# Re-ordering the five queues of a quantised matmul with a layernorm, a base linear layer and LoRA experts, with 83 operations given to another engine

## What is computed

```python
def fake_quant(x, scale, zp):
    q = jnp.clip(jnp.round(x / s + z), QMIN, QMAX)
    return (q - z) * s
x = x + jnp.matmul(fake_quant(_layernorm(x), ...), fake_quant(ctx_4096, ...))
y = _layernorm(x)
base = y @ W_base.T + b_base
lora_out = jnp.einsum('ter,eor,te->to', h, lora_B, w) * SCALING   # h = y @ lora_A, w: top 2 of 8 experts
x = x + base + lora_out
```

## Time and profile before

| | |
|---|---|
| median of 3 runs | 960.43 us (956.87 to 961.31) |
| the profiled execution | 960.41 us, span 958.6 us, granted clock 0.996 |
| TensorE busy | 931.6 us, 97% |
| VectorE busy | 585.5 us, 61% |
| ScalarE busy | 506.9 us, 53% |
| GpSimd busy | 310.2 us, 32% |
| DMA | 197.08 MB, mean 206 GB/s |

### The profile page before, as it was taken

The page is one execution under the profiler, slowest core; times in us unless marked ns, Lnnn a source line. Parts: engine busy times, 40 slices in busy tenths (PEclk is TensorE's granted clock), DMA queues, the critical chain, the costliest instruction groups (busy, mean ns, idle before and its releaser), DMA issues. The chain is left out here.

```text
span 958.6 us, 13081 instructions
## 1 busy us (share of the span) xinstructions
PE 931.6 (97%) x4594; PEld 443.1 (46%) x4614; DVE 585.5 (61%) x729; ACT 506.9 (53%) x495; POOL 310.2 (32%) x249
## 2 busy tenths in 40 slices
...
GB/s 345 412 412 393 219 376 298 299 255 307 293 67 181 198 243 209 221 146 242 200 211 276 181 223 188 345 308 214 117 22 116 50 93 72 98 123 75 85 66 44
DMA packets 61445, 197.08 MB, mean 206 GB/s; under 512 B 5696, under 2 KB 22208, under 8 KB 52928
## 3 DMA queue, kind: packets, MB, share of 16 engines
...
## 5 line engine op out<-in xcount | busy, mean ns | idle before, releaser
L1470 PE MATMUL PS<-XA,Q 128*128 128x512 f16 x384 | 145.6, 379 | 0.0
L1472 PE MATMUL PS<-XA,Q 128*128 128x512 f16 x384 | 145.5, 379 | 0.0
L1471 PE MATMUL PS<-XA,Q 128*128 128x512 f16 x384 | 145.5, 379 | 0.0
L1428 POOL TENSOR_TENSOR S<-S 128x1024 f16<-128x1024 f32 x29 | 64.6, 2233 | 169.4 <-ACT S L1422 169.4
L694 PE MATMUL PS<-Q,S 128*128 128x512 bf16 x501 | 112.7, 383 | 2.2 <-DVE S L709 1.3
L694 PE MATMUL PS<-EX,S 128*128 128x512 bf16 (+1 forms) x535 | 105.7, 354 | 3.5 <-POOL S L674 1.6
L1422 ACT ACTIVATE Q<-S 128x1024 f16<-128x1024 f32 x64 | 66.6, 1050 | 73.2 <-PE PS L1472 29.5
L1470 PE MATMUL PS<-EX,S 128*128 128x512 f16 x256 | 97.0, 379 | 0.5 <-ACT Q L1532 0.5
L1471 PE MATMUL PS<-EX,S 128*128 128x512 f16 x256 | 97.0, 379 | 0.0
L1472 PE MATMUL PS<-EX,S 128*128 128x512 f16 x256 | 97.0, 379 | 0.0
L1377 ACT ACTIVATE S<-S,WC 128x1024 f32<-128x1024 f32 x64 | 70.7, 1137 | 46.1 <-DMA S<-in_wT_dram 31.4
...
## 6 DMA issues: line engine op xcount, KB each, us to landing
...
```

The lines of the kernel that those rows point to most:

```text
L1428: e.tensor_tensor(v[:, 1024:2048], W_SRC[n], v[:, 0:1024], ALU.subtract).then_inc(w_lo.of(i, n), 1)
L1470: e.matmul(bank(bk), wh, yh(op, k), start=(fresh and k == 0), stop=False, skip_group_check=not fresh)
L1471: e.matmul(bank(bk), wh, yl(op, k), start=False, stop=False, skip_group_check=not fresh)
L1472: last = e.matmul(bank(bk), wl, yh(op, k), start=False, stop=(read and k == 7), skip_group_check=not fresh)
```

## The change

sync_first (the first loads) stays. Behind it the queues of all five engines are written in a new order, and 83 operations change engine: w_low (27 from GpSimd to VectorE, 6 the other way), y_low (4 and 17), sqadd0 3, 5, 7 and add0 3, 7, 9 to VectorE, add0 4, 5 to GpSimd; ctx_conv 6, 12, 15, 16, 18, 21, 30 from ScalarE to GpSimd, 4 and 24 from GpSimd and 10 from VectorE to ScalarE; ctx_quant 6 and 10 from ScalarE to VectorE; ln1_back(0,3,0) and (1,4,0) and ln1_quant(1,5) from ScalarE to VectorE, and ln1_back(1,1,0), (1,2,0), (1,5,0), (1,6,0), (1,7,0) and ln1_quant(1,4) from VectorE to ScalarE. No call is added or left out, and TensorE's instructions are the same 4,570 in another order. Two lines shorter, the new file's lines from tensor_program on stand two earlier. The diff, cut:

```diff
-QUANT = {'a': [(0, 0), (0, 2), (0, 3), (0, 4), (0, 5), (0, 6), (0, 7), (1, 1), (1, 2), (1, 3), (1, 5), (1, 6), (1, 7)],
-    'd': [(0, 1), (1, 0), (1, 4)]}
-BACK = {'a': [(0, 0, 0), (0, 1, 0), (0, 2, 0), (0, 3, 1), (0, 3, 0), (0, 4, 0), (0, 5, 0), (0, 6, 0), (0, 7, 0), (1, 0, 0),
-    (1, 3, 0), (1, 4, 0)], 'd': [(0, 7, 1), (1, 1, 0), (1, 2, 0), (1, 5, 0), (1, 6, 0), (1, 7, 0)]}
-CTXQ = {'a': [0, 3, 6, 7, 8, 9, 10, 11, 12, 13, 14, 15, 16, 17, 19, 18, 20, 21, 22, 23, 24, 25, 26, 28, 27, 29, 30, 31],
-    'd': [1, 2, 4, 5]}
-CONV = {'a': [5, 6, 8, 9, 12, 13, 14, 15, 16, 17, 18, 21, 22, 25, 26, 27, 28, 29, 30, 31], 'd': [10, 11, 23], 'p': [0, 1, 2, 3,
-    4, 7, 19, 20, 24]}
+QUANT = {'a': [(0, 0), (0, 2), (0, 3), (0, 4), (0, 5), (0, 6), (0, 7), (1, 1), (1, 2), (1, 3), (1, 4), (1, 6), (1, 7)],
+    'd': [(0, 1), (1, 0), (1, 5)]}
+BACK = {'a': [(0, 0, 0), (0, 1, 0), (0, 2, 0), (0, 3, 1), (0, 4, 0), (0, 5, 0), (0, 6, 0), (0, 7, 0), (1, 0, 0), (1, 1, 0),
+    (1, 2, 0), (1, 3, 0), (1, 5, 0), (1, 6, 0), (1, 7, 0)], 'd': [(0, 3, 0), (0, 7, 1), (1, 4, 0)]}
+CTXQ = {'a': [0, 3, 7, 8, 9, 11, 12, 13, 14, 15, 16, 17, 18, 19, 20, 21, 22, 23, 24, 25, 26, 28, 27, 29, 30, 31], 'd': [1, 2, 4,
+    5, 6, 10]}
+CONV = {'a': [4, 5, 8, 9, 10, 13, 14, 17, 22, 24, 25, 26, 27, 28, 29, 31], 'd': [11, 23], 'p': [0, 1, 2, 3, 6, 7, 12, 15, 16,
+    18, 19, 20, 21, 30]}
...
-SQ0 = {'d': [], 'p': [1, 2, 3, 4, 5, 6, 7, 8, 9, 10, 11, 12, 13, 14, 15]}
-SUM0 = {'d': [4, 5], 'p': [1, 2, 3, 6, 7, 9, 10, 11, 12, 13, 14, 15]}
...
-    (1, 7, '4'), (1, 7, 'T')], 'p': [(0, 0, 'A'), (0, 0, 'T'), (0, 1, 'A'), (0, 2, 'T'), (0, 3, 'T'), (0, 4, 'A'), (0, 6, 'T'),
-    (0, 6, 'A'), (1, 2, 'T')]}
...
-    (15, 5)], 'p': [(0, 6), (0, 2), (0, 5), (1, 2), (1, 5), (1, 6), (2, 2), (2, 6), (2, 5), (3, 2), (3, 5), (3, 6), (4, 2),
-    (4, 6), (5, 2), (5, 6), (6, 2), (6, 6), (7, 6), (7, 2), (8, 1), (8, 0), (8, 4), (8, 2), (8, 3), (8, 6), (8, 5), (9, 3),
-    (9, 2), (10, 2), (10, 3), (11, 3), (11, 2), (12, 2), (12, 3), (13, 3), (13, 2), (14, 3), (14, 2), (15, 2), (15, 3)]}
...
+SQ0 = {'d': [3, 5, 7], 'p': [1, 2, 4, 6, 8, 9, 10, 11, 12, 13, 14, 15]}
+SUM0 = {'d': [3, 7, 9], 'p': [1, 2, 4, 5, 6, 10, 11, 12, 13, 14, 15]}
...
+    (1, 5, '4'), (1, 5, 'T'), (1, 6, 'A'), (1, 6, 'B'), (1, 7, 'A'), (1, 7, 'B'), (1, 7, 'T')], 'p': [(0, 0, 'T'), (0, 0, 'A'),
+    (0, 1, 'T'), (0, 2, 'A'), (0, 2, 'T'), (0, 3, 'A'), (0, 4, 'T'), (0, 4, 'A'), (0, 5, 'A'), (0, 5, 'T'), (0, 7, 'A'),
+    (1, 0, 'A'), (1, 0, '4'), (1, 0, 'B'), (1, 0, 'T'), (1, 2, '4'), (1, 2, 'B'), (1, 2, 'T'), (1, 4, 'B'), (1, 6, '4'),
+    (1, 6, 'T'), (1, 7, '4')]}
...
+    (14, 5), (15, 1), (15, 3), (15, 2), (15, 0), (15, 5), (15, 4), (15, 6)], 'p': [(0, 0), (1, 0), (1, 2), (3, 5), (4, 0),
+    (4, 3), (4, 2), (4, 6), (5, 2), (5, 6), (6, 6), (7, 0), (7, 1), (7, 2), (7, 6), (8, 0), (8, 5), (9, 2), (10, 2), (12, 2)]}
...
-        xn_load(e, 0, 4); xn_load(e, 0, 5); ctx_load(e, 2); xn_load(e, 0, 6); xn_load(e, 0, 7); x_load(e, 0, general)
-        x_load(e, 1, general); xn_load(e, 1, 0); x_load(e, 2, general); ctx_load(e, 3); x_load(e, 5, general)
-        xn_load(e, 1, 1); ctx_load(e, 4); xn_load(e, 1, 2); x_load(e, 6, general); ctx_load(e, 5); x_load(e, 3, general)
-        ctx_load(e, 6); xn_load(e, 1, 3); x_load(e, 9, general); x_load(e, 4, general); xn_load(e, 1, 4); ctx_load(e, 7)
-        r_load(e); ctx_load(e, 8); keep(e, 3); x_load(e, 7, general); xn_load(e, 1, 5); ctx_load(e, 9)
-        x_load(e, 8, general); ctx_load(e, 10); xn_load(e, 1, 6); ctx_load(e, 11); x_load(e, 10, general); ctx_load(e, 12)
-        x_load(e, 12, general); x_load(e, 11, general); keep(e, 2); ctx_load(e, 13); xn_load(e, 1, 7); ctx_load(e, 14)
-        keep(e, 7); keep(e, 0); ctx_load(e, 15); x_load(e, 15, general); keep(e, 1); ctx_load(e, 16); keep(e, 6); keep(e, 5)
...
-        b_load(e, 15); raw_load(e, 15, 0); ob_load(e, 0); ob_load(e, 1); last_store(e, 4); last_store(e, 5)
-        last_store(e, 3); last_store(e, 6)
+        xn_load(e, 0, 4); xn_load(e, 0, 5); ctx_load(e, 2); xn_load(e, 0, 6); xn_load(e, 0, 7); x_load(e, 1, general)
+        x_load(e, 0, general); xn_load(e, 1, 0); ctx_load(e, 3); x_load(e, 2, general); ctx_load(e, 4); xn_load(e, 1, 1)
+        x_load(e, 3, general); x_load(e, 5, general); xn_load(e, 1, 2); ctx_load(e, 5); x_load(e, 7, general)
+        ctx_load(e, 6); xn_load(e, 1, 3); x_load(e, 4, general); ctx_load(e, 7); xn_load(e, 1, 4); x_load(e, 9, general)
+        ctx_load(e, 8); x_load(e, 6, general); x_load(e, 8, general); keep(e, 2); ctx_load(e, 9); xn_load(e, 1, 5)
+        ctx_load(e, 10); x_load(e, 11, general); keep(e, 1); ctx_load(e, 11); x_load(e, 10, general); keep(e, 5)
+        x_load(e, 15, general); xn_load(e, 1, 6); ctx_load(e, 12); ctx_load(e, 13); keep(e, 0); x_load(e, 14, general)
+        x_load(e, 13, general); r_load(e); x_load(e, 12, general); x_load(e, 17, general); ctx_load(e, 14); ctx_load(e, 15)
...
+        raw_load(e, 15, 1); raw_load(e, 15, 0); ob_load(e, 0); ob_load(e, 1); last_store(e, 5); last_store(e, 4)
+        last_store(e, 6); last_store(e, 3)
...
-        gemm1(e, 9, 512, 1024, 0, 8); gemm1(e, 9, 0, 512, 0, 8); gemm1(e, 9, 0, 512, 8, 16); ln1_turn(e, 1, 4)
...
-        gemm1(e, 16, 0, 512, 8, 16); gemm1(e, 16, 512, 1024, 8, 16); a_total(e); mean(e, 0); gemm1(e, 17, 0, 512, 0, 8)
-        gemm1(e, 17, 512, 1024, 0, 8); r_total(e); gemm1(e, 17, 0, 512, 8, 16); gemm1(e, 17, 512, 1024, 8, 16)
-        gemm1(e, 18, 0, 512, 0, 8); gemm1(e, 18, 512, 1024, 0, 8); offset_total(e, 0); offset_total(e, 1)
...
-        gemm1(e, 31, 0, 512, 8, 16); lora_h(e, 0, [0]); w_total(e, 0); lora_h(e, 0, [1]); lora_h(e, 0, [2])
-        lora_h(e, 0, [3]); lora_h(e, 0, [4]); lora_h(e, 0, [5]); lora_h(e, 0, [6]); lora_h(e, 0, [7])
...
+        gemm1(e, 6, 512, 1024, 0, 8); gemm1(e, 6, 0, 512, 8, 16); ln1_turn(e, 1, 4); gemm1(e, 6, 512, 1024, 8, 16)
...
+        gemm1(e, 17, 0, 512, 0, 8); mean(e, 0); a_total(e); gemm1(e, 17, 0, 512, 8, 16); r_total(e)
+        gemm1(e, 17, 512, 1024, 0, 8); gemm1(e, 17, 512, 1024, 8, 16); offset_total(e, 0); gemm1(e, 18, 0, 512, 0, 8)
+        gemm1(e, 18, 0, 512, 8, 16); offset_total(e, 1); gemm1(e, 18, 512, 1024, 0, 8); var_total(e, 0, 0)
+        var_total(e, 0, 1); gemm1(e, 18, 512, 1024, 8, 16); gemm1(e, 19, 0, 512, 0, 8); gemm1(e, 19, 512, 1024, 0, 8)
...
+        w_total(e, 0); lora_h(e, 0, [1]); lora_h(e, 0, [2]); lora_h(e, 0, [3]); lora_h(e, 0, [4]); product(e, 0, 0, 0, 1)
+        product(e, 0, 0, 1, 2); product(e, 0, 0, 2, 3); product(e, 0, 0, 3, 4); product(e, 0, 0, 4, 5); lora_h(e, 0, [5])
+        lora_h(e, 0, [6]); product(e, 0, 0, 5, 6); product(e, 0, 0, 6, 7); product(e, 0, 1, 0, 1); clear(e, 0)
+        lora_h(e, 0, [7]); product(e, 0, 0, 7, 8); mean(e, 1); route(e, 0); product(e, 0, 1, 1, 2); product(e, 0, 3, 0, 1)
...
-        ln1_quant(e, 0, 3); ln1_back(e, 0, 2, 0); ln1_back(e, 0, 3, 1); ln1_back(e, 0, 3, 0); ln1_quant(e, 0, 4)
...
-        post(e, 1, 2); square1(e, 8); post(e, 1, 1); w_squares(e, 2); w_scale(e, 2, 0); w_scale(e, 2, 3); w_scale(e, 2, 2)
...
-        w_high(e, 7, 5); post(e, 7, 2); a_high(e, 1, 0); a_high(e, 1, 1); w_scale(e, 8, 2); w_scale(e, 8, 0)
...
+        square0(e, 0); square0(e, 1); square0(e, 2); square0(e, 3); ctx_conv(e, 10); ctx_quant(e, 12); square0(e, 4)
...
+        w_high(e, 1, 5); copy(e, 1); w_high(e, 1, 6); square1(e, 6); post(e, 1, 2); square1(e, 7); post(e, 1, 1)
...
+        y_high(e, 1, 7, "T"); y_high(e, 1, 7, "4"); post(e, 7, 2); w_scale(e, 8, 2); w_scale(e, 8, 3); w_high(e, 7, 5)
...
+        add0(e, 7); ln1_quant(e, 1, 5); shift0(e, 0); shift0(e, 1); ln1_stats(e, 1, 6); shift0(e, 2); shift0(e, 3)
...
-        y_scale(e, 0, 3, "A"); y_diff3(e, 0, 3); evac1(e, 25, 0); y_diff1(e, 0, 3); evac1(e, 25, 1); add1(e, 9)
...
-        y_diff2(e, 0, 7); y_low(e, 0, 7, "B"); y_diff4(e, 0, 7); y_low(e, 0, 7, "A"); y_low(e, 0, 7, "4"); w_low(e, 0, 0)
-        w_add(e, 0, 1); y_low(e, 0, 7, "T"); lora_sums(e, 0); w_low(e, 0, 1); w_add(e, 0, 2); w_add(e, 0, 4); centre1(e, 0)
...
-        centre1(e, 8); w_norm(e, 2); w_seen(e, 2); w_factors(e, 2); post(e, 1, 4); centre1(e, 9); w_add(e, 2, 1)
...
+        y_scale(e, 0, 7, "A"); y_diff3(e, 0, 7); y_diff1(e, 0, 7); y_diff2(e, 0, 7); w_add(e, 0, 1); y_low(e, 0, 7, "B")
+        y_diff4(e, 0, 7); b_low(e, 0); y_low(e, 0, 7, "4"); y_low(e, 0, 7, "T"); w_low(e, 0, 1); w_add(e, 0, 2)
+        w_add(e, 0, 4); w_low(e, 0, 4); w_low(e, 0, 2); lora_sums(e, 0); w_low(e, 0, 6); centre1(e, 0); w_low(e, 0, 3)
...
+        w_norm(e, 2); w_seen(e, 2); w_factors(e, 2); post(e, 1, 4); centre1(e, 9); w_add(e, 2, 1); w_low(e, 2, 0)
...
-        add0(e, 3); ln1_coef(e, 1, 4); ctx_conv(e, 7); ln1_coef(e, 1, 5); add0(e, 6); add0(e, 7); sqadd0(e, 1); sqadd0(e, 2)
-        sqadd0(e, 3); sqadd0(e, 4); sqadd0(e, 5); sqadd0(e, 6); sqadd0(e, 7); sqadd0(e, 8); ln1_coef(e, 1, 6); add0(e, 9)
...
```

(36 more changed lines are left out.)

549 lines of the change are left out of this document (256 added, 293 removed), and 73 rows, old and new, of tables (EVAC, GEMM, POST, PROD).

## The result

The changed kernel takes 965.61 us (median of 10 executions, 960.13 to 969.4) where the one before takes 960.50 (956.87 to 963.74): a ratio of 1.0059, 95% interval 1.0031 to 1.0086. It is 5 us slower where 5.8 us less had been forecast, and it lies outside the range. The profiled execution took 963.62 us with a span of 961.8, 3.2 more than before's 958.6.

A forecast was written before the change was run, and what follows sets the result against it. TensorE was taken as the bound, busy in 931.6 of 958.6 us. Gains of 9.2 less costs of 3.4 gave 5.8 net, so 960.4 − 5.8 = 954.6 us; range 950.5 to 965, the forecast case's own 951.5 to 958.

The forecast's parts named there:

- All else costs nothing, by cover: Remaining engine moves (w_low, y_low, conversions, sums) in context stretch and products: no cost, as the queues have time to spare.
- The clock, 2.8 us of gain: TensorE's low clock at 160 to 190 and 360 to 370 was to be won back: 1.1 and 1.7 us.
- The second dip: Clock of 0.83 from 360 to 370, taken as gone with the gap directly before it: 1.7 us gained.
- The first, 1.1: Clock of 0.89 and 0.97 at 160 to 190, two chances in three of going as one-column matmuls are spread: 1.1 us.
- the last sign of being wrong: The prediction would be wrong if the clock fell at a new place, 1.7 us each.
- The waits at 365, 285 and 599: TensorE's waits for a norm of W, a low part of y and a post step go: 2.3, 1.2 and 0.7 us gained.
- 160 and 230: TensorE's waits for ctx_conv(18) and for eviction evac1(25,1) go: 0.5 and 1.3 us gained.
- the costs of 71 to 102 and 279 to 293: Context stretch with xn_load(1,6) queued later: 1.1 us (0 to 12); w_low(0,0) on GpSimd: 1.2 us (0 to 3).
- Lead-in 0.3, tail 0.4: ln1_back(0,3,0) ends later on VectorE: 0.3 us; a second last-store issue lies behind the last eviction: 0.4 us.
- The starving DMA: Rival: SP's queue between 70 and 100 starves the context stretch of DMA, 965 to 969 us; chance 0.15.
- The lock: Rival: y_low on GpSimd, 430 to 480, holds off VectorE's two-input operations through shared ports, costing 3 to 5 us; chance 0.14.
- The third rival: The order changes nothing that binds, each wait finds its next releaser: 959 to 961 us; chance 0.05.

The follow-up runs named there:

- e1_stores: Changed kernel with store(7,0) and store(7,1) moved behind w_low(8,0) and w_low(8,5) in GpSimd's queue: 961.18 us, 1.002 against the kernel before.
- e8_stores_mid: Changed kernel with store(7,0) and store(7,1) behind w_low(8,0) only, ahead of w_low(8,5): 960.32 us, 1.0016 against the kernel before.
- e9_stores_tail: Changed kernel with the stores as in e1_stores and last_store(3) ahead of last_store(6) again: 960.82 us, 1.0011 against the kernel before.
- g3: As g2, with store(7,0) and store(7,1) behind w_low(8,5): 963.21 us, 1.0023 against the kernel before.
- g2: Kernel before up to 335 us, then the new order and engines, the two early stores among them: 967.51 us, 1.0081 against the kernel before.
- a0_after: The changed kernel itself measured once more, nothing edited: 967.73 us, 1.009 against the kernel before.
- e5: Kernel before with one edit, store(0,0) ahead of w_low(1,5) in GpSimd's queue: 959.56 us, 1.0007 against the kernel before.
- e5b: Kernel before with store(0,0) ahead of w_low(1,5), measured a second time: 958.47 us, 0.9995 against the kernel before.
- g1: Changed kernel's queues and engines up to 337 us, then the order and engines of before: 961.15 us, 1.0009 against the kernel before.

## Why the prediction was wrong, step by step

The forecast was 5.8 us less and 5.1 more came, 10.9 apart. Two things make it up. One is the cost of two stores, 4.3 to 6.5 us between medians; the other is that the gains did not show in the time: with those stores held back (e1_stores, e8_stores_mid, e9_stores_tail) the new order is 1 to 2 us above the kernel before, not 5.8 below. TensorE's waits of 0.3 us and more, behind the first 30 us, sum to 7.8, 5.6 and 3.9 us in the profiles of these three, and to 5.7 and 7.9 in two profiles of before. The waits that were booked went, and others of about the same size came in their place.

- **The step that failed: "All else costs nothing, by cover"**. The prediction itself says that what changes behind 600 can only lose, and then puts that loss at nothing. It counted the w_low that leave GpSimd by their own durations and asked whether they had time. It did not ask what stood behind them in that queue. Six w_low of block 8 had held stores (7,1), (6,1) and (7,0) back until all y loads but the last had landed; with five of them gone and the sixth behind the stores, two stores of 512 KB share the DMA engines with loads that TensorE is about to want. Price: 2.5 to 4.3 us of waiting in the five profiles that have it, 4.3 to 6.5 us between medians (e1_stores against the changed kernel, g3 against g2). That the stores do it is shown by e8_stores_mid: y_load(2) lands 3.8 us sooner with the stores later and all else equal, and the delay is then on y_load(4). How the DMA engines divide their time between the two is not shown. The medians differ by more than the wait; part of that is the clock. In the profiled execution the low clock behind the wait adds some 1.7 us (15 × 0.08 + 5 × 0.11), in that of a0_after nothing; in the mean of all executions the clock costs 2.2 us in the changed kernel against 1.1 with late stores. The rest is not settled.
- **The clock, 2.8 us of gain: wrong as a sum.** The mean granted clock costs the kernel before 2.1 to 2.6 us (1 minus the clock, times 960, in four sets of 16 to 29 executions beside the experiments) and the changed one 2.2 (14 executions). The second dip, 1.7, was one execution's: the clock in 360 to 370 was 1.00 in the second profile of before, and e5 and e5b, which take away the wait there, still cost 2.2 to 2.5. The first, 1.1, may well have come: with the new context stage and without the early stores (e1, e8, e9 and g1, 42 executions) the clock costs 1.1 us, some 1 less than before. In the changed kernel the early stores bring as much back, and the clock fell at a new place, behind the wait at 627, as the last sign of being wrong had it. Which edit of the context stage does it is not shown.
- **The waits at 365, 285 and 599: gone, as predicted.** None of them is over 0.5 us in a profile of the changed kernel or of e1, e8 and e9. At 365 w_squares(2) of the changed kernel starts at 358.2, not behind a post but behind a raw load that landed just then, where before it started at 360.2. That raw load is the next releaser, which the prediction did not price: in g2 and g3, with the new order from 335 but the old context stage, it lands 1 to 2 us later, and the wait at 365 is 3.0 and 2.7 us, more than the 2.1 of before. So the order of the products does not take the wait away by itself. Also the 2.3 us were one execution's (1.4 in the second profile of before), and e5 and e5b show that taking the wait away alone gives nothing that 24 executions can tell.
- **160 and 230, and the costs of 71 to 102 and 279 to 293:** in sum wrong. The waits at 160 and 230 are gone in both profiles of the changed kernel, and the 1.2 at 279 to 293 did not come as a wait. By 337 the changed kernel was to be 1.9 us ahead (3.4 of waits and 1.1 of clock won, 2.6 spent); TensorE was 2.0 late there in the profile. The wait at 103 was 1.55 us where 1.1 had been allowed, lateness at 115 was 1.9. Not foreseen were 1.56 at 204 (keep(19) queued behind two context loads, its landing at 198.8, x_load(21) behind it) and 0.7 each at 247 and 269. Over executions g1 puts the whole stage at 0.9 us dearer, with an interval of −1.4 to +3.3.
- **Lead-in 0.3, tail 0.4:** TensorE went on at 29.42 instead of 29.27 with a wait of 1.81 for 1.39; the tail cost 0.8.
- **Rivals.** The starving DMA was the right resource at the wrong place: the waits near 103 were small, but the landing of a load hurt at 627. The lock cost TensorE nothing that shows: VectorE's y_low (the form of 23 before, 17 after) has a mean of 1278 ns against 1221, w_low 1268 against 1244, and w_total waits 0.2 us. Single hits there are, 12 two-input operations of VectorE over 1.7 us beside one of GpSimd, 9 before; one falls into 430 to 480, a w_add of 3.04 us at 460.9, where three were feared. The third rival, that each wait finds its next releaser, had 0.05; with late stores it describes what was measured, and in the changed kernel itself the stores come on top.

```profile
L1031 DVE TENSOR_TENSOR S<-S 128x1024 f16<-128x1024 f32 x17 | 21.5, 1278 | 1.3 <-ACT S L992 0.8
...
L1428 DVE TENSOR_TENSOR Q<-S,Q 128x1024 f16<-128x1024 f32 x52 | 65.6, 1268 | 45.1 <-ACT Q L1422 45.1
L1428 POOL TENSOR_TENSOR Q<-S,Q 128x1024 f16<-128x1024 f32 x12 | 26.6, 2220 | 46.8 <-ACT Q L1422 46.8
```

**Left open:** why e1_stores, e8_stores_mid and e9_stores_tail, whose profiles lack before's waits at 285, 365 and 599, still come out 1 to 2 us above it (each interval holds no difference). In the mean their clock costs some 1 us less than before's, so something else must take 2 to 3 us more, an estimate from the two. Part is seen: waits of 0.5 to 1.9 us for the evictions of groups 30 and 31 at 267 to 272, and 0.4 for the gates (the weights w of the experts, which tail waits for) at 324 to 331. What else comes in their longer executions no profile caught.
